# Cross attention on one core: 32x32 turns on VectorE, scores on 16 small TensorE tiles, and part of the softmax on ScalarE straight from PSUM

## What is computed

```
q = split_heads(x @ Wq.T)
for branch in (text, ip):            # 77 keys each
    k, v = split_heads(ctx_b @ Wk_b.T), split_heads(ctx_b @ Wv_b.T)
    probs = softmax(q @ k.T / sqrt(32))
    out += probs @ v
out = merge_heads(out) @ Wo.T + bo + x
```

## Time and profile before

| | |
|---|---|
| median of three runs | 604.17 us (603.97 to 605.0) |
| profiled execution, its own time | 606.17 us |
| its span, first to last instruction | 604.1 us |
| mean granted TensorE clock | 0.991 |
| busy: TensorE, its weight loads | 583.6, 516.3 us |
| busy: VectorE, ScalarE, GpSimd | 445.9, 312.6, 311.0 us |

### The profile page before, as it was taken

The page is one execution under the profiler, slowest core; times in us unless marked ns, Lnnn a source line. Parts: engine busy times, 40 slices in busy tenths (PEclk is TensorE's granted clock), DMA queues, the critical chain, the costliest instruction groups (busy, mean ns, idle before and its releaser), DMA issues.

```text
span 604.1 us, 14571 instructions
## 1 busy us (share of the span) xinstructions
PE 583.6 (97%) x5634; PEld 516.3 (85%) x5634; DVE 445.9 (74%) x576; ACT 312.6 (52%) x594; POOL 311.0 (51%) x341
## 2 busy tenths in 40 slices
PE   8997878999999999999999999999999999999988
PEld 7997757888888888888888888888888888888867
DVE  0028576888788888878888887888888888788872
ACT  0223644565646555565655565555555565645541
POOL 0033436455574656475555647564746555574460
PEclk9998898999999999999999999999999999999999
DMA  8992001112121212112121212121211212111101
GB/s 296 414 374 79 1 1 28 63 36 88 44 81 44 87 35 82 39 46 76 43 87 35 86 39 84 35 87 43 68 53 35 87 35 87 44 37 44 36 18 62
DMA packets 29401, 46.20 MB, mean 76 GB/s; under 512 B 3392, under 2 KB 24512, under 8 KB 29120
## 3 DMA queue, kind: packets, MB, share of 16 engines
q1 hardware_dynamic: 29376, 45.84, 22.3%
HBM read 35.34 MB, written 10.49 MB: 76 GB/s over the span
## 4 chain that ended last, share of the span: by engine, by line
PE 92%; DVE 3%; ACT 2%; DMA 1%; issue 1%; SPq 0%; POOL 0%; ACTq 0%
PE q_ps L580 23%; PE x_ps L580 22%; PE main_ps L616 11%; PE s_ps L604 9%; PE pv_ps L635 8%; PE pv_ps L633 7%; PE s_ps L725 3%; PE pv_ps L624 3%; PE pv_ps L725 2%; PE main_ps L725 1%; DMA stage<-wk_in 1%; DVE row_sum L503 1%; ACT probs L363 1%; PE s_ps L672 1%; ACT p_main L368 1%
## 5 line engine op out<-in xcount | busy, mean ns | idle before, releaser
L305 POOL TENSOR_TENSOR probs<-probs,row_inv 128x616 f32<-128x616 f32 (+1 forms) x160 | 159.7, 1020 | 228.9 <-DVE row_inv L506 228.9
L503 DVE TENSOR_REDUCE row_sum<-probs 128x16 f32<-128x1232 f32 x80 | 114.9, 1436 | 45.7 <-ACT probs L363 45.7
L363 ACT ACTIVATE probs<-probs 128x616 f32<-128x616 f32 x160 | 113.8, 719 | 60.4 <-DVE probs L495 60.4
L368 ACT ACTIVATE p_main<-main_ps 122x512 f32<-122x512 f32 x160 | 94.3, 589 | 88.4 <-PE main_ps L616 88.1
L487 DVE TENSOR_REDUCE row_max<-s_ps 128x16 f32<-128x1232 f32 x80 | 115.3, 1441 | 31.7 <-PE s_ps L604 31.7
L495 DVE TENSOR_TENSOR probs<-s_ps,row_max 128x616 f32<-128x616 f32 x160 | 120.5, 795 | 2.7
L616 PE MATMUL main_ps<-ident,probs 128*122 128x128 f32 x640 | 96.1, 273 | 4.5 <-ACT p_main L368 4.5
L580 PE MATMUL q_ps<-x_hi,wq_hi 128*128 128x256 f32 x400 | 88.9, 320 | 0.0
L387 ACT ACTIVATE attn_hi<-pv_ps 128x256 fp32r<-128x256 f32 x80 | 30.9, 387 | 91.4 <-PE pv_ps L635 91.0
L616 PEld LDWEIGHTS main_ps<-ident,probs 128*122 128x122 f32 x640 | 73.1, 138 | 6.0 <-ACT p_main L368 5.9
L580 PE MATMUL x_ps<-attn_hi,wo_hi 128*128 128x256 f32 x375 | 75.5, 299 | 0.8 <-ACT y L382 0.8
(11 more groups left out here) (71 smaller groups left out, 774.0 us busy)
## 6 DMA issues: line engine op xcount, KB each, us to landing
x_raw<-x_in SPq DMA_DIRECT2D x16, 640.0 KB, 3.8
res<-x_in SPq DMA_DIRECT2D x75, 128.0 KB, 2.0
y_out<-res SPq DMA_DIRECT2D x75, 128.0 KB, 1.7
stage<-wk_in SPq DMA_DIRECT2D x6, 640.0 KB, 8.2
stage<-wv_in SPq DMA_DIRECT2D x6, 640.0 KB, 9.7
wq_raw<-wq_in SPq DMA_DIRECT2D x1, 1600.0 KB, 10.1
wo_raw<-wo_in SPq DMA_DIRECT2D x1, 1600.0 KB, 7.3
stage<-wk_in SPq DMA_DIRECT2D x4, 320.0 KB, 5.8
```

The source lines that it names most:

```text
L305: nc.gpsimd.tensor_tensor(rows[:, :, keys], rows[:, :, keys], row_inv[:, u.slot, :, br].unsqueeze(2) .broadcast_to([P, GROUP * SUB, size]) ...
L363: nc.scalar.activation(probs[:, u.slot, heads], probs[:, u.slot, heads], ACT.Exp).then_inc(exp_done, 1)
L368: nc.scalar.activation(p_main[0:MAIN, :, s * P:(s + 1) * P], main_ps[0:MAIN].rearrange("p (j n) -> p j n", j=GROUP), ACT.Copy).then_inc(ma ...
L503: nc.vector.tensor_reduce(row_sum[:], by_row(probs[:, u.slot].rearrange("p j s n -> p j (s n)")), AXIS.X, ALU.add).then_inc(sum_done, 1)
```

## The change

- **Scores** (`scores`): each matmul now takes 32 queries as the stationary operand (32 rows, 32 columns) and the 77 keys of one branch moving, so that the partitions of the result hold, in quarters, two blocks of 32 queries (halves) times two branches. 64 matmuls per unit on all 16 tiles of 32x32; four spans of 64 queries lie side by side, 77 scores each.
- **Softmax**: `find_max` in two halves with a negated result; for the first two heads ScalarE makes eight activations straight from PSUM, each with the negated maximum as bias and the sum as a second output (`exp_direct`); for the other two the old way stays (`take_max`, `exp`, a sum on VectorE). `invert` runs in two halves, `normalise` on GpSimd in two equal halves.
- **Turning**: no transposes on TensorE in the units. VectorE turns 32x32 blocks, SBUF to SBUF, in two halves (`turn`), 768 elements per partition each, since the 77 keys are padded to 96.
- **Values** (`weigh_values`): for each of three widths of 32 keys, two halves of 64 rows (32 text keys and 32 image keys of one block of queries) times four heads, 24 matmuls on 8 tiles of 64x32, with 128 columns. They accumulate in two PSUM banks.
- `attn_high` and `attn_low` read the two banks with a pattern. The bias waits in addition for the residual addition two chunks back.
- TensorE's order in a unit becomes values(u-2), scores(u), query product(u+2), output product(u-6), and all its units are written out in place of the hardware loop (`unrolled`). VectorE's becomes attn_low(u-2), the two maxima(u), subtraction(u), two turns(u-1), reciprocal, sum, reciprocal(u).
- The start: values are copied into a padded layout by six small copies per engine and branch, and turned in ten rounds of three transposes, placed by ScalarE and VectorE in turn; GpSimd clears the padded arrays first. The matrix v_rest goes.

The diff, cut to its core:

```diff
-            def exp(u, half):
-                heads = slice(half * PAIR, (half + 1) * PAIR)
-                wait(act, s_drained, u.number(2, half + 1))
-                nc.scalar.activation(probs[:, u.slot, heads], probs[:, u.slot, heads], ACT.Exp).then_inc(exp_done, 1)
-
-            def keep_main(u, s):
...
+            def exp_direct(u):
+
+                wait(act, max_done, u.number(2, 1))
+                for j in range(PAIR):
+                    for i in range(SPANS):
+                        done = nc.scalar.activation(probs[:, u.slot, j, i, 0:KEYS], s_ps[:, j, i * KEYS:(i + 1) * KEYS],
+                                                    ACT.Exp, bias=row_neg[:, j, i:i + 1],
+                                                    accum_out=row_sum[:, j, i:i + 1])
+                done.then_inc(direct_done, 1)
+
+            def exp(u):
+                wait(act, sub_done, u.number(1, 1))
+                rows = probs[:, u.slot, heads_of(1), :, 0:KEYS]
+                nc.scalar.activation(rows, rows, ACT.Exp).then_inc(exp_done, 1)
...
                 wait(act, out_ready, c.number(1, 1))
+                wait(act, y_added, c.number(1, -1))
                 nc.scalar.activation(y[:, c.slot, :], x_ps[:, 0:N], ACT.Identity, bias=bo[:, c.g:c.g + 1]).then_inc(y_done, 1)
...
+            def find_max(u, half):
+                if half == 0:
+                    wait(dve, s_ready, u.number(1, 1))
+                nc.vector.tensor_reduce(row_neg[:, heads_of(half)], scores_of(half), AXIS.X, ALU.max, negate=True
                                         ).then_inc(max_done, 1)
...
+            def turn(u, half):
+
+                wait(dve, p_done, u.number(2, half + 1))
+                nc.vector.transpose(turned[:, u.slot, heads_of(half)].rearrange("p j i n -> p (j i n)"),
+                                    probs[:, u.slot, heads_of(half)].rearrange("p j i n -> p (j i n)")
+                                    ).then_inc(p_turned, 1)
+
+            def invert(u, half):
...
             def emit(u):
-                find_max(u)
-                for half in range(2):
-                    take_max(u, half)
                 if u.plus(-2).exists():
                     attn_low(u.plus(-2))
-                invert(u)
-                keep_rest(u.plus(-1))
+                for half in range(2):
+                    find_max(u, half)
+                take_max(u)
+                if u.plus(-1).exists():
+                    for half in range(2):
+                        turn(u.plus(-1), half)
+                for half in range(2):
+                    invert(u, half)
...
             def scores(u):
 
                 wait(pe, q_done, u.number(1, 1))
-                wait(pe, s_drained, u.number(2))
-                for s in range(SUB):
+                wait(pe, direct_done, u.number())
+                wait(pe, sub_done, u.number())
+                for i in range(SPANS):
                     for j in range(GROUP):
-                        done = nc.tensor.matmul(s_ps[:, j, s * BLK:(s + 1) * BLK],
-                                                q[rows_of(j), u.slot, s * P:(s + 1) * P],
-                                                keys[rows_of(j), u.g, u.batch].rearrange("p r n -> p (r n)"),
-                                                start=True, stop=True, skip_group_check=True)
+                        for a in range(GROUP):
+                            h, br = divmod(a, BRANCHES)
+                            first = i * ROWS + h * WIDTH
+                            done = nc.tensor.matmul(s_ps[rows_of(a), j, i * KEYS:(i + 1) * KEYS],
+                                                    q[rows_of(j), u.slot, first:first + WIDTH],
+                                                    keys[rows_of(j), u.g, u.batch, br, :],
+                                                    start=True, stop=True, skip_group_check=True)
                 done.then_inc(s_ready, 1)
...
+            def weigh_values(u):
+
+                wait(pe, p_turned, u.number(2, 2))
                 wait(pe, attn_lo_done, u.number())
...
+                for w in range(WIDTHS):
+                    for h in range(HALVES):
+                        rows = slice(h * ROWS, (h + 1) * ROWS)
+                        for j in range(GROUP):
+                            done = nc.tensor.matmul(by_span(pv_ps[rows_of(j), :, 0:P])[:, h],
+                                                    v[rows, u.g, u.batch, w, rows_of(j)],
+                                                    turned[rows, u.slot, j, :, w * WIDTH:(w + 1) * WIDTH],
+                                                    start=(w == 0), stop=(w == WIDTHS - 1), skip_group_check=True)
+                done.then_inc(pv_ready, 1)
...
             def emit(u):
 
-                last, chunk = u.plus(-1), u.plus(-OUT_LAG)
-                scores(u)
+                chunk = u.plus(-OUT_LAG)
                 if u.plus(-2).exists():
                     weigh_values(u.plus(-2))
+                scores(u)
                 if u.plus(Q_AHEAD).exists():
                     project_q(u.plus(Q_AHEAD))
...
+                if chunk.exists():
+                    project_out(chunk)
...
-            stages(emit, 2)
+            stages(emit, 2, unrolled=True)
```

More of the change, by code:

```diff
@@ L169, in build @@
         consts = sem("consts")
[L170 removed]
+        padded = sem("padded")
         k_acc = sem("k_acc")
@@ L219, in build, with stages @@
         block = stack.enter_context(nc.Block())
-        def stages(emit, first=0):
+        def stages(emit, first=0, unrolled=False):
             def pair(t, first=0):
@@ L226, in stages @@
             pair(0, first)
+            if unrolled:
+                for t in range(1, STEPS):
+                    pair(t)
+                return
             with emit.engine.Fori(1, STEPS - 1) as t:
@@ L334, in emit @@
                 if last.exists():
-                    normalise(last)
-                    normalise_rest(last)
+                    for half in range(2):
+                        normalise(last, half)
                 if chunk.exists():
@@ L343, in _ @@
             split_x(Unit(0, GROUPS))
-            for g in range(GROUPS):
-                rest_of_values(g)
             emit.engine = pool
             stages(emit)
-            normalise(LAST.plus(GROUPS - 1))
-            normalise_rest(LAST.plus(GROUPS - 1))
+            for half in range(2):
+                normalise(LAST.plus(GROUPS - 1), half)
             add_residual(LAST.plus(-2))
@@ L386, in attn_high @@
                 wait(act, pv_ready, u.number(1, 1))
-                nc.scalar.activation(attn_hi[:, u.batch, u.g, :], pv_ps[:, 0:N], ACT.Copy).then_inc(attn_hi_done, 1)
+                nc.scalar.activation(in_halves(attn_hi[:, u.batch, u.g, :]), by_span(pv_ps[:, :, 0:P]), ACT.Copy).then_inc(attn_hi_done, 1)
             def emit(u):
-                ahead, nxt, last = u.tile_plus(2), u.plus(Q_AHEAD), u.plus(-1)
+                ahead, nxt = u.tile_plus(2), u.plus(Q_AHEAD)
                 chunk = u.plus(-OUT_LAG)
@@ L448, in _ @@
             keep_v(1)
-            for g in range(GROUPS):
-                place_v(g)
-            for half in range(2):
-                exp(Unit(0, 1), half)
+            exp_direct(Unit(0, 1))
+            exp(Unit(0, 1))
             keep_q(Unit(0, 2))
-            act.wait_ge(p_zeroed, 1)
-            keep_main(Unit(0, 0), 0)
+            for i in range(0, V_ITEMS, 2):
+                place_v(i)
             for k in range(3, GROUPS):
@@ new lines, in turn @@
+            def turn(u, half):
[4 more added lines that the diff above has]
+            def invert(u, half):
+                if half == 0:
+                    wait(dve, direct_done, u.number(1, 1))
+                else:
+                    wait(dve, exp_done, u.number(1, 1))
+                    nc.vector.tensor_reduce(row_sum[:, heads_of(1)], probs[:, u.slot, heads_of(1), :, 0:KEYS],
+                                            AXIS.X, ALU.add).then_inc(sum_done, 1)
+                    wait(dve, sum_done, u.number(1, 1))
+                nc.vector.reciprocal(row_inv[:, u.slot, heads_of(half)], row_sum[:, heads_of(half)]).then_inc(inv_done, 1)
@@ L565, in _ @@
             attn_low(LAST.plus(GROUPS - 2))
-            keep_rest(LAST.plus(GROUPS - 1))
+            for half in range(2):
+                turn(LAST.plus(GROUPS - 1), half)
             attn_low(LAST.plus(GROUPS - 1))
```

268 lines of the change are left out of this document (97 added, 171 removed).

## The result

The changed kernel takes **687.7 us** (median of 4, 683.6 to 690.9) against 604.6 for the kernel before on the same chip: ratio 1.137, 95% interval 1.130 to 1.145. I had forecast 575, faster. The profiled execution took 683.6, its span is 681.7.

A forecast was written before the change was run, and what follows sets the result against it. TensorE was taken to set the pace at 6.60 us a unit, VectorE's loop afterwards at 6.25: 606.2 - 78 x 0.35 - 2 = 577, less 2.0, 575 us; own range 562 to 600, 8 in 10 560 to 702.

The forecast's parts named there:

- the new chain: Loop of VectorE's maximum, subtraction and turns, then TensorE's values and scores: 6.13 us a unit, 6.25 with x_hi, against 6.60.
- Rival B: VectorE's turns of 32-bit elements go at half rate: 3.5 us instead of 1.85, loop 7.8, 698 us; chance 0.12.
- Rival C: ScalarE becomes the loop: gain gone from 0.39 us per direct activation, 635 us at 0.45; chance 0.13.
- The scores' term: TensorE's 128 score pairs at 6.7 ns each: 0.86 us a unit, plus 0.03 for the first load.
- array bound: Lower bound for TensorE's scores in array time: 128 pairs on 16 tiles are 8 steps of 0.065, 0.52 us.
- rival A: TensorE's score pairs start more slowly than 6.7 ns: gain gone from 9.4 ns, 659 us at 15 ns; chance 0.20.
- Hidden on the mean: TensorE's unrolled instruction traffic, up to 160 packets, one every 3.6 us, each about 1 us long, was taken as hidden.
- rival D: Instruction fetch during TensorE's values and scores: some 0.3 us lost per unit, 6.6 a unit, no change, 604 us; chance 0.05.
- Start and end: Outside the units: v_rest's wait and transposes go, value copies and turning rounds are added; together -2 us.

The follow-up runs named there:

- The bf16 version: The changed kernel with q and keys in bf16, so scores take 64 pairs in place of 128: 559.0 us, ratio 0.927.

## Why the prediction was wrong

It was wrong in direction, by 113 us of the median. By its own steps:

- **VectorE and the new chain held.** Turns 1.83 for two (forecast 1.85), maximum to turned 4.13 (4.15 and 0.05), values 0.87 (0.79). The bf16 version shows the loop at work: 5.88 us. Rival B (698, near the result by chance) is out: turns run at full rate.
- **ScalarE held.** Eight direct activations start every 0.30 us, the forecast value; its rows of 337 and 216 ns overlap. Rival C is out.
- **The scores' term was mis-sized.** 6.7 ns a pair was taken from four tiles in 0.05 us and eight loads, and only the first 32 pairs start that fast; behind them it is 8.3 ns and waits, 10.0 on the mean of 128, 1.28 us. The array bound of 0.52 us, from "77 columns make 0.065", never comes into play: 39 columns take only 0.19 off. This is rival A at 10 ns, just past its break-even of 9.4: 0.42 us a unit, and the whole gain of 0.35 is gone. By my own sum it makes 608, not 688.
- **The decisive step was "Hidden on the mean", and rival D's size.** Its place was right (352 records, packets of 250), but its price of 0.3 us a unit came from comparing the burst with a packet's own 1 us; the packets come at least 3.3 us apart, a stop lasts up to 3.2 us, and the clock falls behind it. Measured: 0.96 us a unit beyond the 6.61, 74 us, of which 56 are the stops and 18 go with the lower clock. I gave it 0.05, and let it cancel the gain alone, where it came on top of rival A.
- **The rules of the Trainium skill.** The start floor of about 25 ns in the Trainium skill's "TensorE: Matmul & The Clock Gate" (Wait — 56ns, not 53.3ns?) is not met on different tiles: 10.0 ns on the mean of 128 pairs, 7.6 in bf16. The Trainium skill, "Runtime: NRT & Kernel Launch" (Instruction fetch mechanics), says that fetching hides behind an issue floor; here 256 instructions pass in 1.3 us, under the 3.3 from packet to packet, and it does not hide.
- **The rest.** Start and end were put at -2 and are +6: the start alone is 5.5 later; which of its steps costs that no run tells. x_hi, forecast at 0.12 a unit, costs nothing here: the fifth units without a stop are 6.61 like the others.

The spans' difference by these: 77 units by 7.57 - 6.64 are 71.5, start and end 6, together 77.5 of 77.6; the median of the runs lies 4 us above the profiled one.

## What to carry to other kernels

Count a change's instructions as well as its array time: where an unrolled engine issues more than one packet's worth (256) in less time than a packet takes to come (3.3 us and more here), it stops, and shortening the work between the stops gave nothing here. Keeping each burst within a packet lessened the stops, but did not end them at the same count. Pairs on small matmul tiles started 8.3 ns apart whatever their columns, so halving their columns saves little and halving their number (one pair for a 16-bit product in place of two for fp32) saves twice, in time and in fetching. An engine freed of work pays only when the loop it leaves is short: with the pairs halved, the same structure went from slower by 14% to faster by 7%, and by 14% once the scores stood ahead of the values.

## What the runs showed of the hardware

Each with its number, none expected: instruction packets never start under 3.25 us apart (17 profiles), and 11 of these kernels stop in the midst of groups, all but once until 1.1 to 1.6 us after a packet has landed. Of the pairs on 32x32 tiles the first 32 start 4 ns apart, the next 8.3, with 39, 77 or 154 columns, in fp32 and in bf16. After a stop of 3.15 us the granted clock is 0.80, then half (0.50) over a window of 1.9 us. A loop of ten units (some 1,300 records) needed 19 packets in all, and the same work written out 45, at no cost in time.
